# A conditioned transformer block on one core: softmax denominators added up over a quarter before the product of ones

## The chip, the core and the metric

The kernel runs on one core of a Trainium2 chip. The metric is the device time of one execution in microseconds (us), lower is better. Three runs of the kernel before gave 3387.61, 3384.66 and 3385.08 us, a median of 3385.08 us.

## The reference

One transformer block with adaptive normalisation, on `x` of 8 x 1024 x 512 in fp32, with 16 heads of 32 channels and a hidden width of 2048:

```python
mod = jax.nn.silu(condition) @ Wada + bada
sh_a, sc_a, gt_a, sh_m, sc_m, gt_m = jnp.split(mod, 6, axis=1)
xm = _layernorm(x, g1, be1) * (1.0 + sc_a[:, None, :]) + sh_a[:, None, :]
x = x + gt_a[:, None, :] * _attention(xm, Wqkv, Wproj, bproj)   # causal, 16 heads
xm = _layernorm(x, g2, be2) * (1.0 + sc_m[:, None, :]) + sh_m[:, None, :]
h = jax.nn.gelu(xm @ W1 + b1, approximate=False)
x = x + gt_m[:, None, :] * (h @ W2 + b2)
# in _attention:
scores = jnp.where(causal, jnp.einsum('bhqd,bhkd->bhqk', q, k) * scale, -jnp.inf)
out = jnp.einsum('bhqk,bhkd->bhqd', jax.nn.softmax(scores, axis=-1), v)
```

The change concerns the denominator of the softmax: for every query and head the sum of the exponentials over all its keys.

## The kernel before

The program has a start (weights split into a high and a low part, the first three blocks of rows projected), a middle part of 16 bodies that does the attention, and a last part that does the output projection and the two big products of the MLP. Only the middle part is changed. It is written as one instruction list for each engine, by hand: `body(u, ...)` walks 40 steps, tables such as `MAX_AT` or `O_COPY_AT` say at which step an engine does what, and semaphores tie the engines together. Every engine takes its list strictly in order.

An **item** is one batch entry with four heads (32 items in all); a body `u` does two of them, steps 0 to 19 the first and 20 to 39 the second. The prediction numbers the steps of a body 0 to 39, and calls the place within an item r, 0 to 19. An item's causal triangle is cut into four quarters of 256 queries, the largest first, and each quarter into tiles of 128 keys: 8, 6, 4 and 2 of them, 20 in all, one a step. Two steps form a **slot**; slots 3, 6, 8 and 9 (`DIAG_SLOTS`) hold the two tiles on the diagonal that close a quarter.

At each step the engines do this:

- TensorE (PE) forms the scores of a tile for four heads (L718), into PSUM tile `psT` (in the last three bodies also a bank of `psA`).
- ScalarE (ACT) exponentiates them (L940) into a ring `e` of 8 tiles. Before it fills a tile it waits on `pv_done`.
- GpSimd (POOL) zeroes what is above the diagonal in `e` (`mask`, L1431) and adds the two exponential tiles of a slot into `es` (`add`, L1449): 128x1024 for a slot off the diagonal, 128x512 for the columns that both tiles of a diagonal slot have.
- PE multiplies the values with the exponentials (`values`, L755), three steps after the exponentials' own, into columns 0 to 255 of `psO`. It multiplies a matrix of ones with `es` into columns 256 to 511 (`added_sums`, L728; in a diagonal slot L760 and L765): that is the sum over keys. Four heads stand side by side, each in 32 columns of the array.
- ACT copies the closed quarter out of `psO` (`o_copy`, L948); SyncE's queue stores the attended rows and the sums.

Beside this the same bodies prepare the **next** item's row maxima: PE forms raw scores in `psS` (`max_item`, L693), VectorE (DVE) masks (L1158) and reduces them (L1162); PE may form the next piece only when the last one is reduced (`max_reduced`). Nine pieces an item, at the odd steps of `MAX_AT`: pieces 3 to 8 at r = 1, 3, 5, 7, 9, 11, pieces 0 to 2 of the following item at r = 15, 17, 19. Then come `max_join` (L1169) at r = 12 and, at r = 13, the transpose on PE (L700).

The first 13 bodies (called with A here) also project a later block of rows: PE's `a_item` (L673, L677), ACT's copy out (`a_copy`, L931), DVE's rounding of queries and keys to their high part (`a_high`, L1145), POOL's low part (`a_low`, L1422), and on DVE the layer norm and, at steps 37, 38, 39 and 0, the split of the modulated rows (`a_split`, L1136 and L1138). The last three bodies have none of this, but POOL and ACT split the MLP's weights in them (`piece_low`, `piece_high`).

## Time and profile before

| what | value |
|---|---|
| median of 3 runs | 3385.08 us |
| the profiled execution's own time | 3385.02 us |
| its span, first to last instruction | 3383.3 us |
| PE busy | 3211.6 us (95%) |
| DVE busy | 2078.7 us (61%) |
| POOL busy | 1557.9 us (46%) |
| ACT busy | 1167.8 us (35%) |
| mean granted TensorE clock | 0.988 |

The first products of values and exponentials start at 192 us, the last at 1674 us: that is the changed part. The bodies with A end at about 1445 us (96.5 us each), the three without take the rest (76 us each). A busy time is the union of an engine's instructions; matmuls overlap by their latency, so what one costs is read from start to start. In a timeline row the bracket is the idle time of that engine ahead of the instruction and what ended it.

### The profile page before, as it was taken

To read this page: it belongs to the slowest core of one execution; us is meant where nothing else is said; L and a number is where in the kernel's file an instruction comes from. 1 tells how busy PE (TensorE), PEld (TensorE's weight loads), DVE (VectorE), ACT (ScalarE), POOL (GpSimd) and SP (SyncE) were. 2 spreads that over 40 slices of the span, in tenths; PEclk is the share of its full clock that TensorE was granted. 3 is DMA by queue.
4 is the path that set the end of the run, shared out by engine and by line. 5 is a ranking of instruction groups with operands and counts; after the bars stand their busy time and mean duration, and the time that the engine had idled before them with its cause. 6 is when DMAs were issued, how large, how long until landed. Compare 5 with 4: busy or idle time off the path is not lost.

```text
span 3383.3 us, 70508 instructions
## 1 busy us (share of the span) xinstructions
PE 3211.6 (95%) x25708; PEld 2581.8 (76%) x25708; DVE 2078.7 (61%) x2511; ACT 1167.8 (35%) x2322; POOL 1557.9 (46%) x1312
## 2 busy tenths in 40 slices
PE   7989999999999999988659999999999999999999
PEld 4656666766666667755458999999999989989898
DVE  5567777767777776676265555555555555555552
ACT  2245555555555555555411111111112112111111
POOL 2246566666666666677652323333223323333232
PEclk9999999999999999999879999999999999999999
DMA  5546565565656555666332223122221222222220
GB/s 213 189 129 185 174 180 171 169 176 167 177 178 184 164 172 175 174 174 169 102 94 74 54 59 74 53 59 68 60 59 60 62 64 53 62 71 53 59 62 13
DMA packets 303514, 391.88 MB, mean 116 GB/s; under 512 B 24240, under 2 KB 206000, under 8 KB 303336
## 3 DMA queue, kind: packets, MB, share of 16 engines
q1 hardware_dynamic: 289904, 367.84, 38.2%
q10 hardware_dynamic: 13440, 21.50, 1.8%
q8 instruction: 140, 2.29, 0.3%
q14 instruction: 30, 0.25, 0.0%
HBM read 270.66 MB, written 118.06 MB: 115 GB/s over the span
## 4 chain that ended last, share of the span: by engine, by line
PE 85%; DVE 9%; issue 3%; ACT 2%; DMA 1%; SPq 0%; DVEq 0%; ACTq 0%; POOL 0%
PE psH L858 22%; PE psY L871 21%; PE psA L677 10%; PE psT L718 7%; PE psA L755 6%; PE psP L837 5%; PE psA L673 4%; DVE mx L1162 4%; PE psS L693 4%; PE psA L728 3%; DVE psS L1158 2%; DVE xm_h L1136 1%; PE psA L646 1%; PE psP L847 1%; PE psT L620 1%
## 5 line engine op out<-in xcount | busy, mean ns | idle before, releaser
L1409 POOL TENSOR_TENSOR h_l<-h_full,h_h 128x256 fp32r<-128x256 f32 x512 | 489.7, 957 | 1120.1 <-DVE h_h L1329 1120.1
L940 ACT ACTIVATE e<-psT 128x512 f32<-128x512 f32 (+1 forms) x1202 | 605.2, 554 | 595.7 <-PE psT L718 593.8
L1449 POOL TENSOR_TENSOR es<-e 128x1024 f32<-128x1024 f32 (+1 forms) x320 | 624.0, 1950 | 392.4 <-PE psA L728 218.5
L1162 DVE TENSOR_REDUCE mx<-psS 128x4 f32<-128x2048 f32 (+3 forms) x384 | 666.1, 1756 | 214.3 <-PE psS L693 207.2
L1037 ACT ACTIVATE h_full<-psH,b1c 128x256 f32<-128x256 f32 x512 | 244.0, 477 | 1332.2 <-PE psH L858 1332.2
L858 PE MATMUL psH<-a_h,w1p_h 128*128 128x256 f32 x2048 | 577.9, 282 | 7.5 <-DVE a_l L1324 7.5
L858 PE MATMUL psH<-a_h,w1p_l 128*128 128x256 f32 x2048 | 580.3, 283 | 0.0
L858 PE MATMUL psH<-a_l,w1p_h 128*128 128x256 f32 x2048 | 579.9, 283 | 0.0
L1329 DVE CAST h_h<-h_full 128x256 fp32r<-128x256 f32 x512 | 148.3, 290 | 536.0 <-ACT h_full L1037 535.0
L718 PEld LDWEIGHTS psT<-qst,kst 97*128 97x128 f32 x2404 | 351.7, 190 | 120.1 <-issue 70.9
L718 PE MATMUL psT<-qst,kst 97*128 97x256 f32 (+1 forms) x2404 | 409.1, 290 | 13.3 <-ACT e L940 11.8
L858 PEld LDWEIGHTS psH<-a_h,w1p_h 128*128 128x128 f32 x2048 | 391.5, 191 | 29.4 <-DVE a_l L1324 7.9
L871 PE MATMUL psY<-w_h,h_h 128*128 128x512 f32 x1024 | 406.8, 397 | 0.0
L858 PEld LDWEIGHTS psH<-a_l,w1p_h 128*128 128x128 f32 x2048 | 391.5, 191 | 19.9
L871 PE MATMUL psY<-w_l,h_h 128*128 128x512 f32 x1024 | 403.5, 394 | 0.0
L871 PE MATMUL psY<-w_h,h_l 128*128 128x512 f32 x1024 | 398.9, 390 | 0.0
L858 PEld LDWEIGHTS psH<-a_h,w1p_l 128*128 128x128 f32 x2048 | 391.5, 191 | 0.0
L1251 DVE RECIPROCAL oin<-oin 128x256 f32<-128x256 f32 x128 | 222.7, 1744 | 231.2 <-DMA oin<-sums 231.2
L755 PE MATMUL psA<-e,vst 128*32 128x256 f32 (+1 forms) x5120 | 312.7, 362 | 4.7 <-ACT o_sb L948 4.0
L1158 DVE TENSOR_TENSOR psS<-psS,mask_q 128x1024 f32<-128x1024 f32 (+1 forms) x160 | 163.0, 1019 | 172.3 <-PE psS L693 172.3
L1422 POOL TENSOR_TENSOR qk_hl<-qk_hl 128x512 fp32r<-128x512 f32 x128 | 173.2, 1353 | 170.9 <-DVE qk_hl L1145 170.9
L755 PEld LDWEIGHTS psA<-e,vst 128*32 128x32 f32 x5120 | 154.6, 110 | 122.0 <-issue 35.0
(113 smaller groups left out, 4762.4 us busy)
## 6 DMA issues: line engine op xcount, KB each, us to landing
qk_split<-qk_hl SPq DMA_DIRECT2D x128, 512.0 KB, 3.4
kst<-qk_split SPq DMA_DIRECT2D x128, 256.0 KB, 4.0
qst<-qk_split SPq DMA_DIRECT2D x128, 256.0 KB, 4.1
xin<-in_x_dram SPq DMA_DIRECT2D x64, 256.0 KB, 4.2
values<-vout ACTq DMA_DIRECT2D x64, 256.0 KB, 4.1
kmx<-qk_split SPq DMA_DIRECT2D x32, 512.0 KB, 4.7
qmx<-qk_split SPq DMA_DIRECT2D x32, 512.0 KB, 6.3
kst<-qk_split SPq DMA_DIRECT2D x128, 128.0 KB, 3.9
```

Of the source, the lines that this page charges most:

```text
L677: mm = pe.matmul(psA[:, bank, :], w[:, k, m * P:(m + 1) * P], a[:, k, :], **ends)
L718: mm = pe.matmul(bank[:, d, 0:w], kst[0:97, hd, key_cols(kt, h)], qst[0:97, q0 // HALF, hd, q0 % HALF:q0 % HALF + w], start=True, stop=Tru ...
L755: mm = pe.matmul(psO[HD * hd:HD * (hd + 1), c:c + w], vst[:, h, kt, HD * hd:HD * (hd + 1)], e[:, (2 * t + d) % ERING, hd, 0:w], start=(kt ...
L858: mm = pe.matmul(psH[:, m % 4, 0:RA], w[:, k, m * P:(m + 1) * P], a[:, par, k, :], start=(n == 0), stop=(n == 3 * KT - 1))
L871: mm = pe.matmul(psY[:, r, :], a[:, m % 4, r * P:(r + 1) * P], w[:, m, :], start=(m == 0 and n == 0), stop=(m == FT - 1 and n == 2), skip_ ...
L940: act.activation(e[:, s % ERING, 2 * hp:2 * hp + 2, 0:w], score_bank(s, hp, with_a)[:, :, 0:w], ACT.Exp, scale=SCALE).then_inc(sem("exp_do ...
L1037: act.activation(h_full[:, m % 4, :], psH[:, m % 4, 0:RA], ACT.Gelu, bias=b1c[:, m:m + 1])\
L1158: dve.tensor_tensor(at, at, mask_q[:].to_broadcast([P, GH, len(chunks), P]), ALU.add)\
L1162: reduce = dve.tensor_reduce(mx[:, part, :, qt], psS[:, :, col:col + w], AX_X, ALU.max)
L1251: dve.reciprocal(oin[:, 1, k], oin[:, 1, k]).then_inc(sem("sums_inverted"), 1)
L1409: return pool.tensor_tensor(dst, full, high.bitcast(F32), ALU.subtract)
L1449: pool.tensor_tensor(to, first, second, ALU.add).then_inc(sem("added"), 1)
```

## The change

The exponentials are no longer handed to the product of ones slot by slot. They are added up in `es` over all key tiles of a quarter; `es` has two buffers and quarter n uses buffer n % 2.

- POOL's `add`: the first slot of a quarter adds two tiles into `es` as before; every later slot off the diagonal adds each of its two tiles to `es`, two instructions with a wait between them; a diagonal slot adds its second tile to columns 128 to 255. There are 13 adds an item where there were 10: nine of 128x1024 (before six) and four of 128x512 (as before).
- DVE's new `join_sums` adds the first tile of the diagonal slot to `es` (128x1024, two SBUF inputs) for three quarters, and copies its first 128 columns (128x512) for the last one, at r = 10, 16, and 0 and 2 of the next item.
- PE's new `sums` is one product of ones a quarter (four heads, 256 columns), after the closing values of the **next** quarter. L728, L760 and L765 go.
- ACT's `o_copy` then takes out this quarter's values with the last quarter's sums; `s_store` stores the sums apart, one quarter later. After the last item there is one more product, copy and store.
- ACT's wait for a free tile of `e` now asks for `pv_done`, `added` and `joined` of the slot that it overwrites.
- `a_high` moves from DVE to ACT, one step after its `a_copy`, behind the step's exponentials.

```diff
+JOIN_SUMS_AT = {10: (0, 0), 16: (0, 1), 0: (1, 2), 2: (1, 3)}
...
+ADDED_BEFORE = [sum(1 if i in DIAG_SLOTS or CHUNKS[2 * i][1] == 0 else 2 for i in range(n)) for n in range(SLOTS + 1)]
+ADDS = ADDED_BEFORE[SLOTS]
+NQ = len(DIAG_SLOTS)
...
-                sp.dma_start(s_dram[bass.ds(hg * GH, GH), cols], o_sb[0:P:HD, n % 2, QUART:2 * QUART])\
-                  .then_inc(o_stored[n % 2], 16)
+                if n > 0:
+                    s_store(u, it, n - 1)
+                elif not (isinstance(u, int) and u == 0 and it == 0):
+                    s_store(u, it - 1, NQ - 1)
+            def s_store(u, it, n):
+                i = u * 2 + it
+                b, hg = i // IPB, i % IPB
+                cols = bass.ds(b * T + QUART * (3 - n), QUART)
+                sp.dma_start(s_dram[bass.ds(hg * GH, GH), cols], o_sb[0:P:HD, (n + 1) % 2, QUART:2 * QUART])\
+                  .then_inc(s_stored[(n + 1) % 2], 16)
...
-            def added_sums(u, t):
-                h, i = divmod(t, SLOTS)
-                pe.wait_ge(sem("added"), (u * 2 + h) * SLOTS + i + 1)
+            def sums(u, it, n, opened):
+                i = u * 2 + it
+                pe.wait_ge(sem("added"), i * ADDS + ADDED_BEFORE[DIAG_SLOTS[n] + 1])
+                pe.wait_ge(sem("joined"), i * NQ + n + 1)
                 past(pe, "pe")
                 for hd in range(GH):
-                    mm = pe.matmul(psO[HD * hd:HD * (hd + 1), QUART:2 * QUART], ones[:],
-                                   es[:, i % SRING, hd, :], start=False, stop=True,
-                                   skip_group_check=True)
+                    mm = pe.matmul(psO[HD * hd:HD * (hd + 1), QUART:2 * QUART], ones[:], es[:, n % SRING, hd, :],
+                                   start=not opened, stop=True, skip_group_check=True)
                 mm.then_inc(sem("summed"), 1)
...
-                    for hd in range(GH):
-                        mm = pe.matmul(psO[HD * hd:HD * (hd + 1), QUART:QUART + P], ones[:],
-                                       e[:, 2 * t % ERING, hd, 0:P], start=False, stop=True, skip_group_check=True)
-                    pe.wait_ge(sem("added"), it * SLOTS + i + 1)
-                    past(pe, "pe")
-                    for hd in range(GH):
-                        mm = pe.matmul(psO[HD * hd:HD * (hd + 1), QUART + P:2 * QUART], ones[:],
-                                       es[:, i % SRING, hd, 0:P], start=False, stop=True, skip_group_check=True)
-                mm.then_inc(sem("pv_done"), 1)
+                    n = DIAG_SLOTS.index(i)
+                    if n > 0:
+                        sums(u, h, n - 1, True)
+                    elif not (isinstance(u, int) and u == 0 and h == 0):
+                        sums(u, h - 1, NQ - 1, True)
...
-                        if t >= 2 and (t - 2) % SLOTS not in DIAG_SLOTS:
-                            added_sums(u, t - 2)
-                        values(u, t - 1)
+                        values(u, s // 2 - 1)
                     if late:
...
...
+            def through(u, t):
+                back, i = divmod(t, SLOTS)
+                it = u * 2 + back
+                wait(act, sem("pv_done"), it * SLOTS + i + 1)
+                wait(act, sem("added"), it * ADDS + ADDED_BEFORE[i + 1])
+                if i in DIAG_SLOTS:
+                    n = DIAG_SLOTS.index(i)
...
...
             def exps(u, s, with_a):
                 c = s % NCH
                 w = CHUNKS[c][3]
                 if s % 2 == 0:
-                    wait(act, sem("pv_done"), u * BODY_SLOTS + s // 2 - 2)
+                    through(u, s // 2 - ERING // 2)
                 for hp in range(2):
                     act.wait_ge(sem("scores_ready"), (u * BODY_STEPS + s) * 2 + hp + 1)
...
                 i = u * 2 + it
-                wait(act, o_stored[n % 2], i * 64 + n // 2 * 32)
-                act.wait_ge(sem("pv_done"), i * SLOTS + LAST_SLOT[3 - n] + 1)
-                act.activation(o_sb[:, n % 2, :], psO, ACT.Copy).then_inc(sem("o_copied"), 1)
+                wait(act, o_stored[n % 2], i * 32 + n // 2 * 16)
+                if isinstance(u, int) and i == 0 and n == 0:
+                    act.wait_ge(sem("pv_done"), LAST_SLOT[3] + 1)
+                    act.activation(o_sb[:, 0, 0:QUART], psO[:, 0:QUART], ACT.Copy).then_inc(sem("o_copied"), 1)
+                else:
+                    wait(act, s_stored[n % 2], i * 32 + n // 2 * 16 - (16 if n % 2 == 0 else 0))
+                    act.wait_ge(sem("summed"), i * NQ + n)
+                    act.activation(o_sb[:, n % 2, :], psO, ACT.Copy).then_inc(sem("o_copied"), 1)
+            def a_high(ia, n):
+                m = n - A_NV
+                act.wait_ge(sem("a_copied"), ia * A_ITEMS + n + 1)
+                act.activation(qk_hl[:, m % QK_RING, HIGH[m // IPB]].bitcast(F32R),
+                               qk_hl[:, m % QK_RING, LOW[m // IPB]], ACT.Copy).then_inc(sem("qk_hi"), 1)
...
+                    item = ended(u, s - 1, with_a, after_a)
+                    if item and item[1] >= A_NV:
+                        a_high(*item)
                     if r in PLACE_AT and not (last and h + PLACE_AT[r][0] == 2):
...
+            act.wait_ge(s_stored[0], 32 * NIT - 16)
+            act.wait_ge(sem("summed"), NIT * NQ)
+            act.activation(o_sb[:, 0, QUART:2 * QUART], psO[:, QUART:2 * QUART], ACT.Copy).then_inc(sem("o_copied"), 1)
...
                 reduce.then_inc(sem("max_reduced"), 1)
+            def join_sums(u, it, n):
+                i = u * 2 + it
+                t = DIAG_SLOTS[n]
+                first = e[:, (it * NCH + 2 * t) % ERING]
+                if n < NQ - 1:
+                    dve.wait_ge(sem("added"), i * ADDS + ADDED_BEFORE[t + 1])
+                    dve.tensor_tensor(es[:, n % SRING], es[:, n % SRING], first, ALU.add).then_inc(sem("joined"), 1)
+                else:
+                    dve.wait_ge(sem("masked"), (i + 1) * len(DIAG))
+                    dve.wait_ge(sem("summed"), i * NQ + n - 1)
+                    dve.tensor_copy(es[:, n % SRING, :, 0:P], first[:, :, 0:P]).then_inc(sem("joined"), 1)
...
+                    if r in JOIN_SUMS_AT:
+                        back, n = JOIN_SUMS_AT[r]
+                        if not (isinstance(u, int) and u == 0 and h < back):
+                            join_sums(u, h - back, n)
...
-                    item = ended(u, s - 1, with_a, after_a)
-                    if item:
-                        a_high(*item)
                     if with_ln and s in LN_STATS_AT:
                         ln_stats(u + AHEAD + 1, LN_STATS_AT.index(s))
...
                 h, i = divmod(t, SLOTS)
-                first, second, to = e[:, 2 * t % ERING], e[:, (2 * t + 1) % ERING], es[:, i % SRING]
+                it = u * 2 + h
+                n = NQ - 1 - CHUNKS[2 * i][0]
+                first, second, to = e[:, 2 * t % ERING], e[:, (2 * t + 1) % ERING], es[:, n % SRING]
+                begins = CHUNKS[2 * i][1] == 0
+                before = it * ADDS + ADDED_BEFORE[i]
                 if i in DIAG_SLOTS:
-                    pool.wait_ge(sem("masked"), (u * 2 + h) * len(DIAG) + 2 * DIAG_SLOTS.index(i) + 2)
-                    first, second, to = first[:, :, P:QUART], second[:, :, 0:P], to[:, :, 0:P]
+                    pool.wait_ge(sem("masked"), it * len(DIAG) + 2 * n + 2)
                 else:
                     pool.wait_ge(sem("exp_done"), (u * BODY_STEPS + 2 * t + 2) * 2)
-                last = (i - SRING) % SLOTS
-                if last in DIAG_SLOTS:
-                    wait(pool, sem("pv_done"), u * BODY_SLOTS + t - SRING + 1)
+                if begins:
+                    wait(pool, sem("summed"), it * NQ + n - 1)
                 else:
-                    wait(pool, sem("summed"), (u * 2 + h) * len(OTHER_SLOTS) + OTHER_SLOTS.index(last) + 1)
+                    pool.wait_ge(sem("added"), before)
                 past(pool, "pool")
-                pool.tensor_tensor(to, first, second, ALU.add).then_inc(sem("added"), 1)
+                if i in DIAG_SLOTS:
+                    other = first if begins else to
+                    pool.tensor_tensor(to[:, :, P:QUART], other[:, :, P:QUART], second[:, :, 0:P], ALU.add)\
+                        .then_inc(sem("added"), 1)
+                elif begins:
+                    pool.tensor_tensor(to, first, second, ALU.add).then_inc(sem("added"), 1)
+                else:
+                    pool.tensor_tensor(to, to, first, ALU.add).then_inc(sem("added"), 1)
+                    pool.wait_ge(sem("added"), before + 1)
+                    past(pool, "pool")
+                    pool.tensor_tensor(to, to, second, ALU.add).then_inc(sem("added"), 1)
             def piece_low(u, q, part):
```

How this moves instructions, at three places.

DVE at the border of two bodies with A. The rows run from the reduction of piece 2 (step 39) over the split of the last quarter of modulated rows (`xm_h`, `xm_l`, step 0) to the masking and first reduction of piece 3 (step 1). Before:

```order
L1162 TENSOR_REDUCE mx<-psS 128x4 [waits max_formed]
L1241 UNCONDITIONAL_BRANCH
L1241 ISA
L1134 REGISTER_ALU [waits a_modulated]
L1136 CAST xm_h<-xin 128x512 [waits a_formed]
L1138 TENSOR_TENSOR xm_l<-xin,xm_h 128x512 [waits xm_hi]
L1144 ISA
L1145 CAST qk_hl<-qk_hl 128x512 [waits a_copied]
L1155 ISA
L1158 TENSOR_TENSOR psS<-psS,mask_q 128x4x2x128 [waits max_formed]
L1160 ISA
L1162 TENSOR_REDUCE mx<-psS 128x4 [waits max_masked]
```

After:

```order
L1211 TENSOR_REDUCE mx<-psS 128x4 [waits max_formed]
L1307 UNCONDITIONAL_BRANCH
L1307 ISA
L1224 TENSOR_TENSOR es<-es,e 128x1024 [waits added]
L1177 ISA
L1183 REGISTER_ALU [waits a_modulated]
L1185 CAST xm_h<-xin 128x512 [waits a_formed]
L1187 TENSOR_TENSOR xm_l<-xin,xm_h 128x512 [waits xm_hi]
L1204 ISA
L1207 TENSOR_TENSOR psS<-psS,mask_q 128x4x2x128 [waits max_formed]
L1209 ISA
L1211 TENSOR_REDUCE mx<-psS 128x4 [waits max_masked]
```

The join (L1224, into `es`) now stands between piece 2 and the split, and the rounding `qk_hl<-qk_hl` (L1145) is gone from in front of piece 3. DVE's own line numbers are those of the changed kernel.

DVE at r = 9 to 12 of the first item of a body with A: piece 7 (two reductions), a statistics instruction of the layer norm, piece 8, and the joining of the maxima. Before:

```order
L1162 TENSOR_REDUCE mx<-psS 128x4 [waits max_masked]
L1162 TENSOR_REDUCE mx<-psS 128x4
L1098 BN_STATS stats<-xin 128x6 [waits x_loaded1]
L1155 REGISTER_ALU
L1162 TENSOR_REDUCE mx<-psS 128x4 [waits max_formed]
L1169 TENSOR_TENSOR mxc<-mx 128x32 [waits max_reduced]
```

After:

```order
L1211 TENSOR_REDUCE mx<-psS 128x4 [waits max_masked]
L1211 TENSOR_REDUCE mx<-psS 128x4
L1223 ISA
L1224 TENSOR_TENSOR es<-es,e 128x1024 [waits added]
L1147 BN_STATS stats<-xin 128x6 [waits x_loaded1]
L1204 REGISTER_ALU
L1211 TENSOR_REDUCE mx<-psS 128x4 [waits max_formed]
L1234 TENSOR_TENSOR mxc<-mx 128x32 [waits max_reduced]
```

The join of the quarter's exponentials stands in front of the statistics and of piece 8.

PE at the end of the first quarter of an item (r = 9): the values of a diagonal slot and what goes with them. Before:

```order
L693 MATMUL psS<-kmx,qmx 128x384 x4
L728 MATMUL psA<-es,ones 32x256 [waits added]
L728 MATMUL psA<-es,ones 32x256 x3
L755 MATMUL psA<-e,vst 32x256 [waits masked]
L755 MATMUL psA<-e,vst 32x256 x3
L755 MATMUL psA<-e,vst 32x128 x4
L760 MATMUL psA<-e,ones 32x128 x4
L765 MATMUL psA<-es,ones 32x128 [waits added]
L765 MATMUL psA<-es,ones 32x128 x3
```

After:

```order
L714 MATMUL psS<-kmx,qmx 128x384 x4
L779 MATMUL psA<-e,vst 32x256 [waits masked]
L779 MATMUL psA<-e,vst 32x256 x3
L779 MATMUL psA<-e,vst 32x128 x4
L753 MATMUL psA<-es,ones 32x256 [waits added,joined]
L753 MATMUL psA<-es,ones 32x256 x3
```

Two ones products of 128 columns go; one of 256 columns takes their place and waits on `added` and `joined`.

## Rows read from the trace of the kernel before

**Rows 1.** Windows: PE, PEld, DVE, ACT, POOL busy, clock, DMA; a stretch with A.

```profile
500.00:700.00 200.00, 193.42 (x1992) 138.42 (x1992) 144.88 (x139) 108.75 (x214) 125.83 (x92) 1.00 0.60 176
```

**Rows 2.** PE's waits, 400 to 1300 us: us in total, times, longest.

```profile
PE psS L693 <- DVE mx L1162: 16.4, 18, 1.2
```

**Rows 3.** Timeline of PE: max pieces at steps 1 to 11, and the transpose.

```profile
775.22 0.56 PE L693 MATMUL psS<-kmx,qmx 32*128 32x128 f32 x8 [1.22 <-DVE mx L1162]
...
780.15 0.51 PE L693 MATMUL psS<-kmx,qmx 32*128 32x512 f32 x4 [0.60 <-DVE mx L1162]
...
785.51 0.50 PE L693 MATMUL psS<-kmx,qmx 32*128 32x256 f32 x8
...
789.84 0.51 PE L693 MATMUL psS<-kmx,qmx 32*128 32x512 f32 x4
...
794.26 0.56 PE L693 MATMUL psS<-kmx,qmx 32*128 32x128 f32 x8
...
799.20 0.51 PE L693 MATMUL psS<-kmx,qmx 32*128 32x512 f32 x4
...
802.77 0.27 PE L700 MATMUL psS<-ident,mxc 128*32 128x128 f32 x1
```

**Rows 4.** Windows over the three bodies without A, their sum.

```profile
sum 229.00, PE 192.29 PEld 124.48 DVE 130.89 ACT 137.33 POOL 174.17; mean PE 64.10 PEld 41.49 DVE 43.63 ACT 45.78 POOL 58.06
```

**Rows 5.** The chain of waits in the bodies without A: start us, us.

```profile
1582.99 2.37 DVE mx L1162 x2
...
1585.96 2.31 DVE mx L1162
```

**Rows 6.** Timeline of PE, r = 19: start us, us, instruction.

```profile
769.74 0.64 PE L728 MATMUL psA<-es,ones 128*32 128x256 f32 x8
770.20 0.83 PE L755 MATMUL psA<-e,vst 128*32 128x256 f32 x16
770.85 0.40 PE L760 MATMUL psA<-e,ones 128*32 128x128 f32 x8
771.07 0.40 PE L765 MATMUL psA<-es,ones 128*32 128x128 f32 x8
771.40 0.74 PE L718 MATMUL psT<-qst,kst 97*128 97x256 f32 x4
```

**Rows 7.** Groups of POOL, DVE, ACT: busy us, mean ns | idle.

```profile
L1449 POOL TENSOR_TENSOR es<-e 128x1024 f32<-128x1024 f32 x190 | 453.0, 2384 | 346.0 <-PE psA L728 213.2 <-ACT e L940 132.7
...
L1145 DVE CAST qk_hl<-qk_hl 128x512 fp32r<-128x512 f32 x104 | 60.8, 585 | 0.0
...
L1138 DVE TENSOR_TENSOR xm_l<-xin,xm_h 128x512 fp32r<-128x512 f32 x48 | 53.6, 1117 | 1.7
...
L948 ACT ACTIVATE o_sb<-psA 128x512 f32<-128x512 f32 x128 | 77.3, 604 | 2.8 <-PE psA L765 2.8
```

**Rows 8.** Groups of DVE: a 128x1024 operation of two SBUF inputs.

```profile
L1258 DVE TENSOR_TENSOR a_full<-oin 128x1024 f32<-128x1024 f32 x32 | 39.5, 1235 | 0.5 <-issue 0.2
```

**Rows 9.** Timeline of DVE around the same body border and first item.

```profile
762.32 1.17 DVE L1145 CAST qk_hl<-qk_hl 128x512 fp32r<-128x512 f32 x1
...
775.53 0.69 DVE L1138 TENSOR_TENSOR xm_l<-xin,xm_h 128x512 fp32r<-128x512 f32 x1
...
777.74 2.36 DVE L1162 TENSOR_REDUCE mx<-psS 128x4 f32<-128x512 f32 x2
...
796.14 2.36 DVE L1162 TENSOR_REDUCE mx<-psS 128x4 f32<-128x512 f32 x2
...
798.41 0.68 DVE L1098 BATCH_NORM_STATS2 stats<-xin 128x6 f32<-128x512 f32 x1
...
799.75 2.29 DVE L1162 TENSOR_REDUCE mx<-psS 128x4 f32<-128x2048 f32 x1 [0.66 <-PE psS L693]
...
802.08 0.52 DVE L1169 TENSOR_TENSOR mxc<-mx 128x32 f32<-128x32 f32 x1
```

**Rows 10.** Timeline of POOL, the add that runs at 762 us.

```profile
760.84 2.36 POOL L1449 TENSOR_TENSOR es<-e 128x1024 f32<-128x1024 f32 x1 [3.31 <-PE psA L728]
```

More of the change, by code:

```diff
@@ L124 @@
 DIAG_SLOTS = [i for i in range(SLOTS) if 2 * i in DIAG]
-OTHER_SLOTS = [i for i in range(SLOTS) if i not in DIAG_SLOTS]
 LAST_SLOT = {CHUNKS[2 * i][0]: i for i in DIAG_SLOTS}
-assert len(CHUNKS) == NCH and SLOTS % SRING == 0
+ADDED_BEFORE = [sum(1 if i in DIAG_SLOTS or CHUNKS[2 * i][1] == 0 else 2 for i in range(n)) for n in range(SLOTS + 1)]
+ADDS = ADDED_BEFORE[SLOTS]
+NQ = len(DIAG_SLOTS)
+assert len(CHUNKS) == NCH and NQ == 4
 assert sorted((qt, part) for chunks, _ in MAXES for qt, part, _, _ in chunks) == \
@@ L295, in build @@
         o_stored = [sem(f"o_stored{s}") for s in range(2)]
+        s_stored = [sem(f"s_stored{s}") for s in range(2)]
         A_NLO = A_NQK
```

18 lines of the change are left out of this document (14 added, 4 removed).

## The prediction

> **What bounds the kernel now.** I read the busy windows first. In the bodies with A, PE is busy 193.42 of 200 us at the full granted clock, DVE 144.88, POOL 125.83, ACT 108.75 [rows 1]: PE bounds, at 97%, with DVE at 72% and POOL at 63%. Then PE's waits: 400 to 1300 us hold a little over nine such bodies, and the only wait that matters is 16.4 us in 18 pieces for DVE's reduced maxima, two a body [rows 2]. The timeline shows where: steps 1 and 3 of a body, behind the border, idle 1.22 and 0.60 us [rows 3]. In the three bodies without A, PE is busy 192.29 of 229 us and POOL 174.17 [rows 4]; there the chain of waits runs through DVE's reductions: one piece ends at 1582.99 + 2.37 = 1585.36 and the next starts at 1585.96, the 0.60 us being PE's own 0.5 us of raw scores [rows 5].
>
> **What goes from PE.** Start to start, a product of ones over 256 columns for four heads takes 770.20 - 769.74 = 0.46 us, one over 128 columns 771.07 - 770.85 = 0.22 us; the second of the pair takes 0.33 us to the scores, of which I count 0.22, since the last product before the scores pays the 0.11 us turn in either kernel [rows 6]. An item has six of the long and eight of the short: 6 x 0.46 + 8 x 0.22 = 4.52 us. It keeps four long ones, 1.84 us. Gone: 2.68 us an item, 5.36 us a body with A, 69.7 us for 13 of them and 16.1 us for the last six items. PE bounds where A runs, so all of the 69.7 us would come if nothing else moved.
>
> **What is added.** POOL gets three adds of 2.384 us an item, 7.15 us [rows 7]. With A it is busy 0.63 x 48.2 = 30.3 us of an item and would be at 37.5 of some 47: it has room, and the ring of eight tiles gives its adds about six steps (14 us) before ACT wants the tile again, so ACT's wider wait costs nothing there. Its low parts of queries and keys come earlier, since ACT now rounds them. ACT takes eight roundings a body of about 0.6 us, as its other 512-column copies [rows 7]; it is idle 46% of the time, and where it is just behind PE I allow nothing for it.
> DVE loses eight roundings of 0.585 us a body [rows 7] and gets six joins and two half-size copies. No row shows a join. From below it is 1.235 us, a 128x1024 operation with two SBUF inputs when the engine is not disturbed [rows 8]. From above: the split's subtraction, of the same kind at half the size, takes 0.69 us when alone [rows 9] but 1.117 us on average [rows 7], and a cast at 762.32 took 1.17 us where the mean of its group is 0.585: it ended at 763.49, just behind POOL's add that ran from 760.84 to 763.20 [rows 9, 10]. So the end of the range is 1.235 plus a whole add of 2.36, 3.6 us. I take 1.8 us: 1.235 and 0.6 us, the subtraction's excess of 0.43 us a little enlarged because POOL will be busy 80% and not 63%.
>
> **A rule against the change.** The cast and the add look as if one waited for the other [rows 9, 10]. The Trainium skill, "SBUF — State Buffer", section "SBUF: two separate sides", says that GpSimd and a VectorE operation with two SBUF inputs share one pair of ports as an exclusive lock, and that the loser is fully blocked. Taken whole, a join meets an add that is running four times in five and waits half of it: 0.8 x 1.19 = 0.95 us, so 2.2 us and not 1.8. By that the sum below would end near 3376 us, and it is the mechanism of rival B.
>
> **Where the joins stand on PE's path.** PE forms a max piece only when the last one is reduced, so DVE's order matters at three places.
> 1. The border, each body. PE reaches step 1 only when piece 2 is reduced (the 1.22 us wait [rows 3]), so the 0.44 us saved at step 39 is lost. Behind it the join (1.8 us) comes in front of the split and of piece 3, a rounding (0.58 us) goes: piece 3 ends 1.2 us later than 777.74 + 2.36 = 780.10, which is what PE waited for at 780.15 [rows 3, 9]. Loss: 1.6 us. The sums of step 1 wait for the same join, but end before PE's wait at step 3.
> 2. Steps 5 to 7 of either item. A masked piece takes DVE from PE's start to reduced 798.50 - 794.26 = 4.24 us (piece 7 [rows 3, 9]); PE comes back after 4.33 us, 785.51 to 789.84 [rows 3]. Of the 0.46 us saved only 0.1 can be used. With small change elsewhere, loss: 0.3 us an item, 0.6 a body.
> 3. Piece 8. In the first item DVE is free at 798.50, works off 0.68 us of statistics and starts piece 8 at 799.75; it ends at 802.04, the maxima are joined at 802.60, and PE's transpose follows at 802.77 [rows 3, 9]: no slack. With the join first, piece 8 starts at 798.50 + 1.8 + 0.68 = 801.0, 1.2 us later, and the 0.44 us saved at step 9 goes too. Loss: 1.65 us. In the second item there is no statistics instruction and a rounding goes; I count nothing.
> Left: 5.36 - 1.6 - 0.6 - 1.65 = 1.5 us a body, 19.6 us in 13.
>
> **The bodies without A.** From step 1 to 13 DVE is on the path, so what PE saves at 5, 7 and 9 does nothing. The join in front of piece 8 has a hole of 0.60 us [rows 5] and delays it by 1.2 us; steps 13, 15 and 19 give back 0.46 + 0.44 + 0.44 = 1.34 us. That is 0.1 us for five items. The last item has no maxima, so most of its 2.68 us comes: 2 us. Together about -2.5 us. POOL goes from 174.17 to 217.1 us of 229 [rows 4], close to full but not over.
>
> **The end.** The last quarter's sums need one more product (0.46 us) and one more copy (about 0.6 us by the old one [rows 7]), while that quarter's values end 0.4 us earlier: +1 us.
>
> **Sum.** The profiled execution took 3385.0 us, 1.7 us outside its span, and is the median of the runs to 0.1 us. 3385.0 - 19.6 - 2.5 + 1 = 3363.9, so 3364 us.
>
> **Rivals.**
> A. PE keeps nearly all of its gain. For it: DVE is idle 28% and PE waits for it in two places a body only; if a join runs in 1.24 us and the holes around it shift with PE, the three losses shrink to tenths. Against: the rows show no slack at the border and at piece 8 [rows 3, 9]. Time: 3385 - 69.7 - 7 (half of the late share) + 1 = 3309 us.
> B. The joins cost PE more than the ones products did. A join waits for the add that POOL runs, and stands in front of a max piece; PE waits for the piece. For it: the cast behind the add [rows 9, 10], and POOL busier than ever. Each further 1 us on a join costs about 1 us at the border, 1 at piece 8 of the first item and a quarter in the second: 2.25 us a body. The 1.5 us left are used up at a join of 1.8 + 0.67 = 2.5 us; from there the kernel is slower. At 3.0 us: 2.7 - 1.5 = +1.2 us a body, +16 for 13, and +6 in five late items; 3385 + 16 + 6 - 2.5 + 1 = 3405 us. Against: the subtraction, under the same disturbance, lost only 0.43 us.
> C. POOL becomes the bound without A. 217.1 us of work, and of the 55 us that it idled there a third stays (masks wait for exponentials, the second add for the first): 235 us, 6 us more than now. Its late adds then hold up DVE's joins. Time: 3385 - 19.6 + 6 + 1 = 3372 us.
>
> **Chances.** The forecast 0.47, A 0.20, C 0.17, B 0.16. A measurement tells 0.2%, some 6.8 us, from no change. Faster by more: 0.44 of the forecast, all of A, 0.10 of C, 0.74. Within: 0.03, 0.05 of C, 0.05 of B, 0.13. Slower: 0.02 of C and 0.11 of B, 0.13. The range of 8 in 10 runs from 3325 us, half way into A, to 3392, which leaves out most of B. The forecast's own is 3348 to 3378 us: joins of 1.24 us at the border and at piece 8 give 1.1 us a body more, 15 us, joins of 2.2 us take 12 us.
>
> **What would show it.** PE's busy time in the middle part falls by 86 us or near it, while a body with A shrinks by only 1.5 us, to 95 us, and PE's waits for L1162's successor grow from 1.8 us a body to about 5, at steps 3, 7 and 13 of the first item. The transpose of step 13 shows idle time of more than 1 us. DVE's join has a mean of 1.6 to 2.0 us; under 1.4 speaks for A, above 2.5 for B. POOL has nine long adds an item and is busy 78 to 82% with A. The three late bodies stay within 5 us of 229; if they grow while POOL is over 95%, it is C. ACT waits for nothing of POOL or DVE. I am wrong if bodies with A lose more than 3 us each, or if PE waits for the sums' join and not for the maxima.

## The result and the profile after

The changed kernel takes 3481.07 us (median of 4 runs, 3472.11 to 3488.79), the one before 3385.03 us: a ratio of 1.0281, 95% interval 1.0253 to 1.0310. It is 2.8% slower, 96 us, where 21 us less was forecast. The profiled execution took 3476.49 us, and its 91 us more stand in two stages, 89 of them. The part from the first product of values to the last piece of A ("with A" below) goes from 1253.8 to 1306.1 us, the three bodies without A ("late") from 227.9 to 264.9 us.

Windows of the kernel after, columns as in [rows 1]: the same stretch, the whole part with A, and the bodies without A.

```profile
500.00:700.00 200.00, 183.82 (x1600) 127.54 (x1592) 158.77 (x135) 112.50 (x224) 157.09 (x103) 0.97 0.57 169
...
193.00:1499.00 1306.00, 1197.94 (x10317) 828.39 (x10313) 1021.00 (x847) 723.30 (x1437) 1010.43 (x656) 0.96 0.56 165
1499.00:1764.00 265.00, 219.71 (x1911) 133.46 (x1913) 168.57 (x119) 137.62 (x279) 229.28 (x152) 0.79 0.45 128
```

The same two stages in the kernel before, whose late one covers what [rows 4] sums:

```profile
192.00:1446.00 1254.00, 1212.67 (x12384) 865.36 (x12384) 897.36 (x848) 678.06 (x1334) 793.26 (x580) 1.00 0.59 172
1446.00:1674.00 228.00, 191.29 (x2406) 123.66 (x2408) 130.42 (x94) 136.59 (x278) 173.17 (x132) 0.99 0.54 147
```

Take PE's column against the length. With A, PE does 2067 instructions fewer, worth 69.7 us by the prediction's prices, and its busy time falls by only 14.7 us (1212.67 to 1197.94), while its idle time goes from 41 to 108 us. Without A, 495 instructions fewer go with 28 us more of busy time (191.29 to 219.71). The column behind POOL's says why: the granted clock, the share of 2.4 GHz, went from 1.00 to 0.96 and from 0.99 to 0.79. By that column (1.00 - 0.96) x 1306 = 52 and (0.99 - 0.79) x 265 = 53 us of full speed are missing, an estimate of the right size for both.

PE's waits of the kernel after, 400 to 1300 us, which answers [rows 2]; with them a wait of ACT:

```profile
ACT e L970 <- POOL es L1522: 21.5, 6, 3.8
...
PE psS L714 <- DVE mx L1211: 20.7, 37, 1.3
PE psS L721 <- DVE mxc L1234: 20.2, 9, 2.2
```

To the wait for maxima (37 times for 18) comes one for the joined maxima (`mxc`), once a body. ACT's wait is looked into under a_unroll.

The chain of waits through a body's border (start us, us, what) answers [rows 3, 9]; L1224 is the join, L753 the product of ones:

```profile
788.80 2.62 DVE es L1224
791.42 0.79 DVE xm_h L1185
...
793.80 2.28 DVE mx L1211
796.08 0.71 DVE xm_h L1185
...
799.83 2.29 DVE mx L1211
802.11 0.04 issue
802.16 0.55 PE psS L714 x7
802.71 0.79 PE psA L779 x16
803.50 0.90 issue
804.40 1.08 PE psA L753 x8
805.48 1.15 PE psT L739 x4
806.63 2.56 PE psA L694 x6
```

DVE sets the pace from 788.80 to 802.11 us. PE idles in front of the maxima and of the sums, which wait for a second join (802.03 to 804.30 us of DVE's timeline), and then runs slower. PE's timeline shows the change of level (the last number in brackets is the idle time):

```profile
798.37 0.40 PE L694 MATMUL psA<-wqkv_h,xm_h 128*128 128x512 f32 x1
798.60 0.40 PE L694 MATMUL psA<-wqkv_l,xm_h 128*128 128x512 f32 x1
...
800.42 0.99 PE L739 MATMUL psT<-qst,kst 97*128 97x256 f32 x4 [0.49 <-ACT e L970]
802.16 0.55 PE L714 MATMUL psS<-kmx,qmx 32*128 32x128 f32 x8 [0.75 <-DVE mx L1211]
...
804.40 1.08 PE L753 MATMUL psA<-es,ones 128*32 128x256 f32 x8 [0.90 <-issue]
...
806.43 0.63 PE L694 MATMUL psA<-wqkv_h,xm_h 128*128 128x512 f32 x1
806.86 0.63 PE L694 MATMUL psA<-wqkv_l,xm_h 128*128 128x512 f32 x1
```

The same product follows its neighbour after 0.23 us, and behind the three gaps after 0.43 us, which is the level of 1.2 GHz. It lasts to 811.6 us. The first of the three gaps is put down to ACT, which stood still for 3.65 us before 799.77 us.

What holds up a join shows when its times are laid beside POOL's. DVE's timeline, then POOL's:

```profile
788.80 2.62 DVE L1224 TENSOR_TENSOR es<-es,e 128x1024 f32<-128x1024 f32 x1
...
832.01 2.11 DVE L1234 TENSOR_TENSOR mxc<-mx 128x32 f32<-128x32 f32 x1
```

```profile
787.97 2.37 POOL L1525 TENSOR_TENSOR es<-e 128x1024 f32<-128x1024 f32 x1 [0.64 <-PE psA L753]
...
831.74 2.34 POOL L1530 TENSOR_TENSOR es<-es,e 128x1024 f32<-128x1024 f32 x1 [0.18 <-POOL es L1527]
```

This add is the group of [rows 7]; the join answers to [rows 8], and both lines to what stood in [rows 9, 10]. The join ends 1.08 us behind the add (791.42 against 790.34), and the tiny joining of maxima, begun 0.27 us behind an add, ends 0.04 us behind its end. Of the 96 joins 69 begin while POOL runs a two-input operation (61 times an add into `es`, 8 times a low part); 68 of them end 1.07 to 1.16 us after it. The views of the two lines give shortest, median and longest in ns:

```profile
L1224 DVE TENSOR_TENSOR es<-es,e x96: 1207/1320/3267, 215.5 to 1758.9; 128x1024 f32<-128x1024 f32 x96
...
L1234 DVE TENSOR_TENSOR mxc<-mx x32: 179/1291/2122, 176.0 to 1705.2; 128x32 f32<-128x32 f32 x32
```

In the kernel before, the second had this row:

```profile
L1169 DVE TENSOR_TENSOR mxc<-mx x32: 177/521/747, 175.7 to 1627.5; 128x32 f32<-128x32 f32 x32
```

Nearly all of these tiny instructions, 31 of 32 before and 30 of 32 after, begin during an add of POOL and end 0.05 to 0.1 us behind it. What changed is how much of the add is still to run when they begin.

The Trainium skill, "SBUF — State Buffer", section "SBUF: two separate sides", calls this an exclusive lock of the ports that GpSimd and VectorE share; by that rule all these ends agree. The masking of maxima, whose tile is in PSUM, doesn't show it: of its 155, 104 begin during a two-input operation of POOL, and 60 of these end before it does.

In the bodies without A the chain of waits looks like this, for [rows 5]:

```profile
1564.21 2.36 DVE mx L1211 x2
1566.56 3.18 DVE es L1224
1569.75 2.21 DVE mx L1211
1572.62 1.87 PE psA L779 x16
```

A join of 3.18 us stands between two reductions, and sixteen products of values take 1.87 us, where they took 0.86 us at the full clock (796.57 us of PE's timeline). PE's waits between 1499 and 1764 us hold one on POOL's masks (L1499) that the kernel before doesn't have in its late bodies:

```profile
PE psA L779 <- POOL e L1499: 10.1, 7, 4.3
```

### The profile page after: what moved, and what is told of

Its sections match the earlier page's. It is cut to its first block, busy times and chain, and to the rows that moved or that the text cites. A ratio compares the mean times of both kernels' runs of the same rounds, so it can differ in the third digit from the quotient of the medians.

```text
span 3474.7 us, 66019 instructions
## 1 busy us (share of the span) xinstructions
PE 3228.0 (93%) x23148; PEld 2555.4 (74%) x23148; DVE 2239.1 (64%) x2535; ACT 1213.1 (35%) x2427; POOL 1830.2 (53%) x1408
## 4 chain that ended last, share of the span: by engine, by line
PE 72%; DVE 18%; issue 6%; DMA 1%; ACT 1%; POOL 1%; SPq 0%; DVEq 0%; ACTq 0%; POOLq 0%
PE psH L878 21%; PE psY L891 20%; DVE mx L1211 8%; PE psA L698 7%; PE psP L857 5%; PE psA L779 5%; PE psT L739 4%; PE psA L694 3%; DVE es L1224 3%; PE psS L714 3%; DVE psS L1207 2%; DVE xm_h L1185 1%; DVE mxc L1234 1%; PE psP L867 1%; PE psA L753 1%
## 5 line engine op out<-in xcount | busy, mean ns | idle before, releaser
L739 PEld LDWEIGHTS psT<-qst,kst 97*128 97x128 f32 x2404 | 374.1, 202 | 159.1 <-issue 96.9
L739 PE MATMUL psT<-qst,kst 97*128 97x256 f32 (+1 forms) x2404 | 436.0, 303 | 17.6 <-ACT e L970 12.5
L779 PE MATMUL psA<-e,vst 128*32 128x256 f32 (+1 forms) x5120 | 344.6, 390 | 22.4 <-POOL e L1499 18.3
L1525 POOL TENSOR_TENSOR es<-e 128x1024 f32<-128x1024 f32 x96 | 232.9, 2426 | 164.2 <-PE psA L753 147.9
L1527 POOL TENSOR_TENSOR es<-es,e 128x1024 f32<-128x1024 f32 x96 | 230.1, 2397 | 89.6 <-ACT e L970 86.0
L779 PEld LDWEIGHTS psA<-e,vst 128*32 128x32 f32 x5120 | 142.9, 114 | 156.0 <-issue 100.3
```

The lines of the kernel that those rows point to most:

```text
L739: mm = pe.matmul(bank[:, d, 0:w], kst[0:97, hd, key_cols(kt, h)], qst[0:97, q0 // HALF, hd, q0 % HALF:q0 % HALF + w], start=True, stop=Tru ...
L779: mm = pe.matmul(psO[HD * hd:HD * (hd + 1), c:c + w], vst[:, h, kt, HD * hd:HD * (hd + 1)], e[:, (2 * t + d) % ERING, hd, 0:w], start=(kt ...
L1525: pool.tensor_tensor(to, first, second, ALU.add).then_inc(sem("added"), 1)
L1527: pool.tensor_tensor(to, to, first, ALU.add).then_inc(sem("added"), 1)
```

## The experiments

Times are medians, and each ratio is to the kernel before as it was timed beside that kernel (3385.0 to 3387.1 us); "with A" and "late" are the two stages of the profiled run alone, the clock beside each. q14 is the number of blocks of instructions that ACT's queue loaded between 500 and 1300 us.

| kernel | us | ratio (95% interval) | with A | late | q14 |
|---|---|---|---|---|---|
| before | 3385.0 | | 1253.8, 1.00 | 227.9, .99 | 0 |
| after | 3481.1 | 1.0281 (1.0253, 1.0310) | 1306.1, .96 | 264.9, .79 | 38 |
| a_unroll | 3439.1 | 1.0163 (1.0144, 1.0182) | 1278.2, .98 | 258.6, .84 | 11 |
| b_ahigh | 3466.1 | 1.0238 (1.0221, 1.0255) | 1300.7, .98 | 264.2, .82 | 37 |
| c_join | 3364.8 | 0.9944 (0.9927, 0.9961) | 1202.2, .99 | 254.0, .83 | 42 |
| d_add | 3430.1 | 1.0134 (1.0113, 1.0154) | 1272.7, .98 | 249.8, .84 | 40 |
| e_all | 3348.5 | 0.9887 (0.9871, 0.9904) | 1209.2, .99 | 233.0, .89 | 12 |
| f_noones | 3320.0 | 0.9806 (0.9789, 0.9822) | 1193.3, .98 | 221.9, .91 | 0 |
| g_pad | 3386.7 | 0.9999 (0.9989, 1.0009) | 1253.9, 1.00 | 227.9, .99 | 40 |
| h_fill | 3495.3 | 1.0327 (1.0310, 1.0344) | 1328.3, .98 | 261.1, .87 | 38 |
| i_align | 3441.6 | 1.0168 (1.0151, 1.0185) | 1278.2, .98 | 258.2, .82 | 0 |
| j_move | 3422.1 | 1.0113 (1.0096, 1.0129) | 1248.1, .99 | 269.0, .79 | 12 |
| k_direct | 3391.1 | 1.0014 (1.0004, 1.0023) | 1232.2, 1.00 | 250.4, .92 | 10 |
| l_mixed | 3362.4 | 0.9933 (0.9916, 0.9949) | 1231.8, 1.00 | 226.1, 1.00 | 10 |

**a_unroll.** ACT's loop is written out.

```
-            with act.Fori(1, NU - AHEAD - 1) as u:
+            for u in range(1, NU - AHEAD - 1):
```

> The changed kernel with ScalarE's loop over the bodies written out (body 1 to 11), nothing else. Theories for the 96 us: T1, instruction loading: ScalarE's loop body became longer and its sequencer now loads instructions anew at each turn of the loop (the instruction queue moves five blocks a body where it moved none), which holds ScalarE some 3.7 us at the border of each body. T2, the joins in front of the maxima on VectorE. T3, GpSimd is full in the three late bodies. T4, TensorE, less full, falls to 1.2 GHz more often, and that multiplies each hole. By T1 ScalarE's waits at the border go (33.5 us in nine), the clock falls less often in the bodies with A, and the time is 3395 to 3435 us; late bodies stay at 267 us. By T2, T3 or T4 alone the time stays within 10 us of 3480.

42 us less, just outside what T1 gave, and late 6 us less where no change was said. ACT's wait "<- POOL es L1522" is gone, though POOL does what it did: that wait was put down to the semaphore that came last, while ACT in fact stood at the end of its loop. In its place stands one on POOL's second add, once a body, which nothing here puts a price on:

```profile
ACT e L970 <- POOL es L1530: 16.7, 9, 1.9
```

Writing the loop out also takes away most of ACT's counting of semaphore values (517 instructions of its sequencer for 1596 in 500 to 1300 us). i_align below keeps the loop and comes to the same time.

**b_ahigh.** DVE rounds the queries and keys again, as in the kernel before.

```
 (ACT)  -   if item and item[1] >= A_NV: a_high(*item)
 (DVE)  +   if item: a_high(*item)
```

> The changed kernel with the rounding of queries and keys (a_high) back on VectorE, where it stood before. By T1 (instruction loading on ScalarE) its loop is shorter by eight copies and their waits; if that is enough to fit again, the five loaded blocks a body vanish and the time falls to 3400 to 3440 us. By T2 (VectorE bounds PE through the maxima) VectorE gets 4.7 us a body more and the time rises by 10 to 30 us to 3490 to 3510.

15 us less, where T1 gave 40 to 80 us less and T2 10 to 30 us more: neither came. T1's condition wasn't met, since the loop is still 306 instructions long and the loading stays at 37 blocks. That DVE gets eight roundings a body more and the kernel is no slower speaks against reading T2 as DVE's mere load; why it is faster wasn't looked into. In the waits of 400 to 1300 us ACT's now carries its right name:

```profile
ACT e L970 <- issue: 28.7, 6, 5.0
```

**c_join.** Each join works on one column a head, and so does the last quarter's copy (not in the lines below), so that nearly all of the first tile is left out of the sums.

```
-dve.tensor_tensor(es[:, n % SRING], es[:, n % SRING], first, ALU.add)
+dve.tensor_tensor(es[:, n % SRING, :, 0:1], es[:, n % SRING, :, 0:1], first[:, :, 0:1], ALU.add)
```

> The changed kernel with VectorE's joins cut to one column a head; every wait and the order stay (the sums lack the first diagonal tile). By T2 this gives back what the joins cost on the maxima's path: 3.85 us a body with A by my own sum, 50 us, and 1.2 us in each late item, so 3410 to 3435 us. By T1 and T3 it gives less than 20 us, 3460 us or more.

116 us less, 104 of them with A: the largest of the single edits, 8 us a body, about twice what I had put on the joins. PE's busy time with A falls from 1197.9 to 1156.4 us, though it does the same products: 42 of the 104 us are the clock, which is back at .99, and the rest is idle time. PE's waits in 400 to 1300 us:

```profile
PE psS L714 <- DVE mx L1211: 5.1, 19, 0.3
```

**d_add.** The first of a slot's two adds works on one column a head; the rest of that tile is left out.

```
-pool.tensor_tensor(to, to, first, ALU.add)
+pool.tensor_tensor(to[:, :, 0:1], to[:, :, 0:1], first[:, :, 0:1], ALU.add)
```

> The changed kernel with the first of the two adds of a later slot cut to one column a head: GpSimd does nine adds of some size as before, with the waits of the change (the sums lack three tiles an item). By T3 the three late bodies fall from 267 to 225 to 235 us and the bodies with A hardly change: 3435 to 3450 us. By T1 and T2 under 15 us are gained, except that joins wait less for GpSimd's adds (at most 0.5 us each).

51 us less, 33 with A and 15 late. T3, which wanted the late bodies at 225 to 235 us and no change with A, isn't borne out as it stood. With A the changed kernel's POOL was not full (1010.43 of 1306 us, 77%); a shorter add holds fewer instructions of DVE. Waits of 400 to 1300 us:

```profile
PE psS L721 <- DVE mxc L1234: 8.7, 18, 0.7
```

That wait was 20.2 us with a longest of 2.2.

**e_all.** The three edits a, c and d together.

> The changed kernel with all three at once: ScalarE's loop written out, joins cut to one column, the first of two adds cut to one column (sums incomplete). What is left is the removal of the ones products, with all new waits. If T1, T2 and T3 are the whole story, the bodies with A take 1190 us (1254 - 66) and the late ones about 215 us, 3305 us in all. If T4 is a cause of its own (TensorE, with less to do where it does not bound, stays at 1.2 GHz), the late bodies stay over 235 us and the total is 3330 us or more.

133 us less, where the three alone add to 209: they take away the same waits. With A it is no faster than c_join alone (1209.2 for 1202.2 us), so with short joins neither ACT's stop nor the first adds cost anything there. Neither forecast fits whole: late it is 233 us, just under the 235 of T4, and the total is over its 3330. What is left of the change without these costs is some 39 us under the kernel before.

**f_noones.** The kernel before, its products of ones cut to one column of one head (and the first of a diagonal slot's two, not shown below, gone); the sums are nearly all left out.

```
-for hd in range(GH): mm = pe.matmul(psO[..., QUART:2 * QUART], ones[:], es[:, i % SRING, hd, :], ...)
+for hd in range(1):  mm = pe.matmul(psO[..., QUART:QUART + 1], ones[:], es[:, i % SRING, hd, 0:1], ...)
```

> The kernel before with its products of ones cut to one column of one head (sums wrong), adds and waits as they were: only PE's saving, larger than the change's (about 4.3 us an item instead of 2.68). My prediction's sum would give 13 x (8.6 - 0.6 - some 1.5 us at the border) = 85 us less with A and 8 us less in the late bodies, 3292 us. T4 says that the late bodies, where PE does not bound, get slower through a lower clock: late part above 235 us instead of 228, granted clock there below 0.9 instead of 0.99, total 3305 to 3325 us.

65 us less, 60.5 with A and 6 late. Products priced at 26 x 4.52 = 118 us with A gave back half: PE's busy time there fell by 77 us (1212.67 to 1135.79) at a clock of .98, and its idle time grew by 17. So taking work away lowers the clock even without a join or an add more. T4's forecast for the late bodies was wrong, though: they came to 221.9 us and not over 235, at .91. Less work alone doesn't make them longer. This is about the most that thinning these products could bring, before anything is paid for it.

**g_pad.** The kernel before with 60 empty semaphore increments in ACT's loop.

```
+if not isinstance(u, int):
+    for _ in range(1 + s % 2):
+        act.sem_inc(sem("pad_act"), 1)
```

> The kernel before with 60 empty semaphore increments a body in ScalarE's loop over the bodies. They do no work; they make the loop as long as the changed one and a little longer. T1: the instruction queue moves blocks in every body, ScalarE is held about 4 us at each border, PE's clock falls behind it: the bodies with A take 30 to 60 us more, 3415 to 3445 us. If loading is harmless: 3385 to 3390 us (60 increments are at most 3 us a body on an engine that is idle 46%).

No change, 3386.7 us, although the loading is there (waits, 400 to 1300 us):

```profile
ACT e L940 <- issue: 29.9, 9, 3.8
```

So ACT's stop of up to 3.8 us a body costs nothing in the kernel before and some 40 us in the changed one (a_unroll, i_align). It is no price of its own, but one paid where the joins already stand: with short joins it is free again (c_join against e_all).

**h_fill.** The changed kernel with 12 of an item's 40 score products done twice, for the same result.

```
-for d in range(2):
+for d in (0, 1, 0, 1) if hp == 1 and s % 5 < 3 else range(2):
```

> The changed kernel with 12 of an item's 40 score products formed twice into the same place (2.8 us more PE work an item, the result is the same): PE gets back the work that the change took from it. T4: the granted clock rises, 0.79 to over 0.9 in the late bodies, and the late part falls below 255 us from 265 although PE has more to do; in total within 15 us of 3481. Without T4 each item pays the 2.8 us where PE bounds: 3481 + 40 to 60 = 3520 to 3540 us.

14 us more in all, which is T4's "within 15"; its clock of over .9 and its 255 us for the late bodies were not reached. Late, where PE waits for others, the added work made the stage 4 us shorter, at a clock of .87 for .79. With A the added products, 12 x 26 by the 0.24 us of half a step (785.00 to 785.48 us), are at most 75 us and cost 22. With more to do PE got the higher clock here, but filling it doesn't pay.

**i_align.** 92 empty increments on ACT in front of its loop, which moves it and leaves its length.

```
+for _ in range(92):
+    act.sem_inc(sem("pad_act"), 1)
 with act.Fori(1, NU - AHEAD - 1) as u:
```

> The changed kernel with 92 empty semaphore increments on ACT before its loop of bodies, so that the loop's 315 instructions begin at number 384 of ACT's program in place of 292 and end at 698 in place of 606. If what decides the loading at the loop's turn is only how long the loop is (306 and more were loaded anew, 273 not), this changes nothing: 37 to 40 blocks on the queue q14 between 500 and 1300 us, ACT's hold at each border, 3476 to 3486 us. If it is where its two ends lie in the blocks of 128 instructions, the loading can go (0 to 5 blocks) and the time goes to what the loop written out gave, 3434 to 3450 us. I hold the first for likelier, 2 to 1.

3441.6 us and no block loaded between 500 and 1300 us: the less likely of my two readings. Length alone doesn't decide. ACT's instructions take 64 bytes in the compiled program and a block on q14 is 8 KiB (0.31 MB by 38), 128 instructions; a_unroll agrees, which runs 1418 of them in these 800 us and loads 11 blocks. The numbers that follow are places in ACT's compiled program. The loops that stay loaded end 41 (before, 281 to 553) and 58 instructions (here, 384 to 698) into their block, those that don't at 78 (b_ahigh, 285 to 590), 94 (after, 292 to 606) and 101 (g_pad, 281 to 613); all lie in three blocks. That fits a load of the next block which starts somewhere between 58 and 78 and drops the loop's first; that is a guess at the cause, and where exactly wasn't tried. The Trainium skill, "Runtime: NRT & Kernel Launch", section "Instruction fetch mechanics", says that a taken branch whose target lies outside the two loaded pages forces a fetch before execution goes on. The kind of stop agrees; the page's 16 KiB blocks don't, since this queue moved 8 KiB ones.

**j_move.** ACT's loop written out, and two joins moved.

```
-JOIN_SUMS_AT = {10: (0, 0), 16: (0, 1), 0: (1, 2), 2: (1, 3)}
+JOIN_SUMS_AT = {13: (0, 0), 16: (0, 1), 0: (1, 2), 4: (1, 3)}
```

> The changed kernel with ACT's loop written out and two of the four joins an item moved on DVE: the first from step 10 to step 13 (behind the pieces of steps 9 and 11), the fourth from step 2 to step 4 (behind the piece of step 3). Theory of the joins (they cost because DVE's pieces, and with them PE's next maxima, stand behind them): the waits of PE for mx in the part with A fall, and the time falls against the kernel with the loop alone written out (3439 us) by 10 to 30 us, to 3410 to 3430. Rival (the joins cost because DVE and POOL have no room left at all, wherever they stand): 3432 to 3447.

17 us less than a_unroll, inside the theory's range: 30 with A, but 10 us more late. My reason was wrong in part: the wait for mx did not fall (38.6 us for 30.2). What fell is the wait of the transpose for the joined maxima, 20.2 us, which is no longer among the waits of 400 to 1300 us: with the join behind piece 8, the joining of maxima takes 0.53 us in the median of 400 to 1300 us, for 1.70 in a_unroll. The join at step 13 is behind the last piece, and the next lines show what it holds instead:

```profile
ACT e L970 <- DVE es L1224: 25.9, 10, 2.6
```

**k_direct.** From the kernel before: POOL adds over the quarter, but nothing is joined. At the diagonal slot PE multiplies ones by the first tile and by the sum, 28 products an item in place of 40 (the changed kernel: 16), counted as 256 columns of one head. `a_high` stays on DVE and ACT's loop is written out; against the changed kernel more than the joins differs.

```
+if i in DIAG_SLOTS[:3] and adds_up(u):
+    for hd in range(GH):
+        mm = pe.matmul(psO[..., QUART:2 * QUART], ones[:], e[:, 2 * t % ERING, hd, :], start=False, ...)
+    pe.wait_ge(sem("added"), it * SLOTS + i + 1)
+    for hd in range(GH):
+        mm = pe.matmul(psO[..., QUART:2 * QUART], ones[:], es[:, DIAG_SLOTS.index(i) % SRING, hd, :], ...)
```

> The kernel before with the adding up over a quarter, but without a join and without standing a quarter behind: POOL adds as in the changed kernel (3 more adds an item), and at a quarter's diagonal slot PE multiplies ones by the first tile and by the sum (28 products an item in place of 40; the changed kernel has 16). ACT's loop written out, a_high on DVE as before. It is a kernel that computes the reference. Theory that the joins on DVE are the largest cost: against the changed kernel the part with A falls from 1306 to about 1235 to 1250, DVE's pieces are on time as before, but the late bodies stay long (POOL 229 of 250 us and more there): 250 to 262 us; sum 3385 to 3405. Rival (POOL's adds are the cost wherever they are made): the part with A stays above 1265 and the total above 3420.

3391.1 us. With A it is 22 us under the kernel before, 74 under the changed one and 46 under a_unroll, with the same three adds more on POOL. Late it is 250.4 us, without a join:

```profile
1424.00:1674.00 250.00, 198.79 (x2101) 122.00 (x2103) 131.93 (x94) 136.52 (x278) 214.91 (x150) 0.92 0.48 133
```

POOL is busy 214.91 of 250 us, the clock is at 0.92, and PE waits for POOL's masks in these 250 us:

```profile
PE psA L763 <- POOL e L1451: 11.7, 7, 4.2
```

**l_mixed.** The same with `LATE = 13` for 16: the last three bodies add as before.

> As the one without joins, but the last three bodies, which have no A items and in which POOL was at 173 of 228 us before, add as before (one add a slot, 40 products of ones an item). Theory: part with A 1235 to 1250 as there, late bodies back at 226 to 232 with the clock at .97 or more, total 3363 to 3382, below the kernel before by up to 0.6 percent. Rival (also in the bodies with A POOL's three more adds cost more than 12 products of ones gave back): part with A above 1254, total 3387 to 3420.

3362.4 us, the version that beats both: 0.67% under the kernel before, just below the range of the theory and far from its rival. Its two stages:

```profile
192.00:1424.00 1232.00, 1182.96 (x11142) 827.25 (x11139) 914.94 (x848) 673.26 (x1334) 978.65 (x657) 1.00 0.60 175
1424.00:1650.00 226.00, 188.22 (x2391) 121.71 (x2393) 130.47 (x94) 136.56 (x278) 173.03 (x133) 1.00 0.53 148
```

An item drops 4.52 - (6 x 0.46 + 2 x 0.22) = 1.32 us of products, 34 us for 26, and PE's busy time falls by 29.7: at a clock of 1.00 the prediction's prices nearly hold, and the stage gains 22. The kernel before with ACT's loop written out and nothing else wasn't run; since it loads nothing, and g_pad's loading cost nothing, little of the 22 us can be that. POOL is busy 978.65 of 1232 us, 79%, and PE and ACT wait 2.5 us for it in all. The joining of maxima is as short as in the kernel before, although POOL is as busy as in the changed one:

```profile
L1189 DVE TENSOR_TENSOR mxc<-mx x26: 472/524/534, 218.6 to 1410.3; 128x32 f32<-128x32 f32 x26
```

## Why the prediction was wrong

The forecast's range ended at 3392 us, and slower had a chance of 0.13. The sign "bodies with A lose more than 3 us each" came: they lost 4.0.

**What goes from PE: the failed step.** The prices of products are right, but the sum takes the full 5.36 us a body and sets only waits against it; for PE's clock it has nothing. PE's busy time with A fell by 14.7 us and not by 69.7; 55 us, 4.2 a body, went into the lower clock. The stretch at 798 to 807 us shows the fall behind three gaps. In c_join, where most of the gaps are gone, 42 us of busy time come back, and the clock is at 1.00 in k_direct and l_mixed, which take fewer products away and add little idle time (49 us with A in both, for 41). Late the same holds: 191.29 - 16.1 = 175 us of work took 219.71, 44 us for the clock. The balance of both stages: 99 us for the clock and 75 us of idle time more, less the 86 us of products, is the 89 us that they grew by.

**Joins: price right, path too cheap.** The forecast was 1.8 us, the mean is 158.7 us by 96, 1.65 us. Their effect was put at 3.85 us a body. PE's idle time grew by (108 - 41) / 13 = 5.1, some of it by ACT's stop, and taking the joins away gives 8.0 us a body, clock and all. Missed was that a join isn't the only one held: behind it the joining of the maxima, right in front of PE's transpose, comes early in an add of POOL in place of late, and goes from 0.52 to 1.29 us in the median. It is the shifted order that does this and not POOL's share (77% with A, forecast 78 to 82), since k_direct and l_mixed have that share and 0.52 us. The place "piece 8" was right, and the forecast idle time of over 1 us in front of the transpose is 2.24 us. At the border shown the forecast wait at step 3 isn't there: the piece starts at 809.98 us, behind DVE's 808.90, because PE had already lost the time to the gaps and the clock. PE's waits for maxima came to 4.5 us a body (40.9 by 9), against 5 forecast. The rule of the lock, priced at 2.2 us a join, would still have given 3376.

**ACT "costs nothing".** Wrong. The longer loop is loaded anew at each turn, which costs 42 us by a_unroll (28 with A in the profiled runs). g_pad shows that the same stop is free in the kernel before. "ACT waits for nothing of POOL or DVE" is wrong as well, once the stop no longer hides it: 16.7 us for POOL's second add in a_unroll.

**The bodies without A.** Forecast -2.5 us, rival C +6, measured +37. C named the right engine: POOL is busy 229.28 of 265 us, PE waits 10.1 us for its masks, and in k_direct, which has POOL's adds and no joins, PE waits 11.7 for them and the late bodies take 22 us more than before. d_add takes 15 us off; l_mixed, whose late bodies are the old ones, is back at 226. But C put POOL at 217.1 us, its sign of over 95% didn't come (87%), and it left out the clock.

**The end.** +1 us was forecast. Behind the last values the kernel after takes 3474.7 - 1764.0 = 1710.7 us of its span, the kernel before 3383.3 - 1674.1 = 1709.2: +1.5.

**Rivals.** A fell. B's side was right and its threshold not: slower from a join of 2.5 us was said, and it is slower at 1.65. Its 3405 us fell 76 short, as it too had no clock, no stop of ACT and late bodies nearly unchanged. Of the single edits to the changed kernel only c_join, with short joins, is faster than before.

**Open.** How the 96 us divide can't be said, since the edits overlap (209 us alone, 133 together). What of the time late is POOL itself and what the clock that follows from PE's waiting isn't separated either; h_fill bounds it from below only, at 4 us and the work added. That the clock fell because of the gaps is read from their order in time and from runs where both go together; no run changed one without the other. j_move's 10 us more late weren't looked into.

## What to carry to other kernels

Work taken off a full TensorE is worth its price only if no gap comes in its place: price the granted clock of the stretch first, since here the clock that fell behind gaps of 0.5 to 0.9 us took 4.2 us a body. Look in the profile of before for small two-input instructions of DVE that end just behind an add of POOL. Whatever moves them to an earlier point of the add lengthens them (0.52 to 1.29 us), and the one in front of PE's next product counts. Apply such a trade stage by stage: without the joins, the same adds and fewer products gain 22 us where POOL goes to 79% busy and lose 22 where it goes to 86%.

## What the runs showed of the hardware

- A DVE instruction with two inputs in SBUF that begins during a two-input operation of POOL waits for its end: 68 of 69 joins ended 1.07 to 1.16 us behind it. A tiny one pays the same wait, up to 2.1 us for 128x32. Masks on a tile in PSUM didn't: 60 of 104 ended first.
- ACT's loop of 315 instructions was loaded anew each turn (38 blocks in 800 us, a stop of up to 3.8 us) or not at all, by where it lies in the program: 3481.1 or 3441.6 us. In the kernel before the same stop cost nothing (3386.7 us).
- With fewer products PE can be busy longer: 495 instructions fewer and 28 us more, at a granted clock of 0.79, in bodies where it also waited for POOL and DVE. Products away alone (f_noones) brought .91 and 10 us less busy time.
